# Thirty-two images through a fused network on one core: the first five turns written out in an order of their own, and the next to last pair normalised and scaled in three groups of tiles

## What is computed

```python
def forward(x, ...):                                  # token network, 192 channels, 14x14 patches
    loc = conv(x, pl_w, pl_b, stride=PATCH)
    loc = dwconv(gelu(loc), pl_dw, pl_pw, pl_pwb)     # layer "L"
    g = wavelet_packet(x)
    g = gelu(conv(g, pg_w1, pg_b1))
    g = gelu(dwconv(g, pg_dw, pg_pw, pg_pwb))         # layer "G"
    glob = conv(g, pg_w2, pg_b2)                      # "W2"
    gate = 0.5 * (jnp.tanh(alpha) + 1.0)
    h = (1.0 - gate) * loc + gate * glob
    h = jax.nn.relu(dwconv(h, f1_dw, f1_pw, f1_pwb))  # "F1"
    h = jax.nn.relu(dwconv(h, f2_dw, f2_pw, f2_pwb))  # "F2"
    h = dwconv(loc + h, f3_dw, f3_pw, f3_pwb)         # "F3"
    ...                                               # layer norm over the channels, class token in front
h = jnp.concatenate([tokens(x), txt], axis=1)         # 1 + 196 + 128 tokens of 192
h = h + attention(_layernorm(h))
h = h + ffn(_layernorm(h))

def attention(x):
    q = mlp(x, qw1, qb1, qw2, qb2)                    # k and v alike, gelu inside
    scores = jnp.einsum('bid,bjd->bij', q, k) / SCALE
    scores = scores * mask                            # 0 <= i - j < 64, no softmax
    y = jnp.einsum('bij,bjd->bid', scores, v)
    ...                                               # layer norm with ln_w, ln_b

def bitlinear(x, w, g):                               # used twice in the FFN: 192 -> 2x512, silu gate, 512 -> 192
    x_norm = rmsnorm(x, g)
    x_q = activation_quant(x_norm)                    # round(x * 127 / max|x|) per token
    return jnp.einsum('bsd,od->bso', x_q, weight_quant(w))   # weights -1, 0, 1 times a scale
```

## Time and profile before

| what | us |
| --- | --- |
| median of three runs | 1143.92 |
| lowest and highest | 1141.91, 1146.18 |
| the profiled execution, its own time | 1147.13 |
| its span in the profile | 1145.3 |

### The profile page before, as it was taken

One profiled execution on the slowest core, in us unless ns is written; L12 is line 12 of the kernel. 1 busy time (PEld: TensorE's weight loads), 2 busy tenths in 40 slices (PEclk: granted clock), 3 DMA queues, 4 the chain that ended last, 5 costly groups with the idle time before them and its releaser, 6 DMA issues.

```text
span 1145.3 us, 19061 instructions
## 1 busy us (share of the span) xinstructions
PE 1059.6 (93%) x5641; PEld 700.3 (61%) x5691; DVE 976.4 (85%) x2829; ACT 881.8 (77%) x2173; POOL 792.1 (69%) x916
## 2 busy tenths in 40 slices
PE   6887999999999999999999999999999989888865
PEld 4554667666757575766666675757676666454522
DVE  0678868999989898999999998989899999666786
ACT  3446758697979888898979798988889787738545
POOL 4245475878787787878787778877787887646334
PEclk9888999999999999999999999999999999979988
DMA  8111010101001010101010100101010000000000
GB/s 342 43 50 40 4 50 4 50 5 58 13 22 49 11 59 10 60 11 60 7 61 5 33 38 19 51 10 60 11 60 10 18 9 12 8 16 16 16 16 22
DMA packets 23687, 41.14 MB, mean 36 GB/s; under 512 B 3649, under 2 KB 20385, under 8 KB 21281
## 3 DMA queue, kind: packets, MB, share of 16 engines
q1 hardware_dynamic: 23584, 39.93, 10.3%
HBM read 31.02 MB, written 7.99 MB: 34 GB/s over the span
## 4 chain that ended last, share of the span: by engine, by line
PE 53%; ACT 22%; DVE 16%; issue 4%; POOL 3%; DMA 2%; SPq 1%; DVEq 0%; POOLq 0%; ACTq 0%
PE bank L558 10%; PE bank L590 4%; ACT xh L1265 4%; PE bank L592 3%; PE bank L601 3%; PE bank L652 3%; ACT y_sb L1274 3%; DVE bank L1953 3%; PE bank L600 3%; ACT early L1251 2%; PE bank L776 2%; PE bank L536 2%; PE bank L708 2%; PE bank L537 2%; PE bank L654 2%
## 5 line engine op out<-in xcount | busy, mean ns | idle before, releaser
L1953 DVE SCALAR_TENSOR_TENSOR bank<-padA,c_col,bank 128x406 f32<-128x406 f32 x560 | 358.5, 640 | 9.1
L558 PE MATMUL bank<-x_sb,w_emb 128*128 128x392 f32 x576 | 221.1, 513 | 6.1 <-ACT padA L1201 3.1
L1251 ACT ACTIVATE prod<-padB,c_col 128x196 f32<-128x196 f32 x432 | 175.4, 451 | 4.9 <-DVE padB L1965 3.9
L558 PEld LDWEIGHTS bank<-x_sb,w_emb 128*128 128x128 f32 x576 | 102.0, 194 | 64.1 <-issue 12.6
L3045 POOL TENSOR_TENSOR yg<-y_f,c_gout 128x512 f32<-128x512 f32 (+2 forms) x73 | 92.9, 1273 | 52.5 <-DVE y_f L2234 52.2
L1251 ACT ACTIVATE early<-padB,c_col 128x196 f32<-128x196 f32 x288 | 118.9, 449 | 3.7 <-POOL accB L3079 3.6
L536 PE MATMUL bank<-accA,w_sq 128*128 128x196 f32 x256 | 66.5, 341 | 11.8 <-POOL accB L3079 6.8
L2214 DVE SCALAR_TENSOR_TENSOR ya<-th,bank 128x512 f32<-128x512 f32 (+2 forms) x73 | 49.9, 684 | 28.7 <-ACT th L1323 27.4
L708 PE MATMUL bank<-w_in,xq 128*128 128x512 bf16 (+2 forms) x252 | 67.1, 382 | 5.1 <-ACT xq L1317 2.4
L590 PE MATMUL bank<-xT,w_sq 128*128 128x325 f32 x192 | 64.4, 447 | 4.0 <-ACT hq L1209 3.9
L3064 POOL TENSOR_TENSOR prod<-prod 128x392 f32<-128x392 f32 x48 | 48.9, 1018 | 27.8 <-ACT prod L1251 27.7
(11 more groups left out here) (320 smaller groups left out, 3015.7 us busy)
## 6 DMA issues: line engine op xcount, KB each, us to landing
x_sb<-xt SPq DMA_DIRECT2D x16, 1176.0 KB, 5.2
out<-o_sb SPq DMA_DIRECT2D x64, 96.0 KB, 1.9
w_sq<-squares SPq DMA_DIRECT2D x1, 3840.0 KB, 15.9
h_sb<-txt SPq DMA_DIRECT2D x32, 51.8 KB
out<-o_sb SPq DMA_DIRECT2D x32, 48.0 KB, 1.9
h_sb<-txt SPq DMA_DIRECT2D x32, 44.2 KB
w_in<-win SPq DMA_DIRECT2D x1, 1024.0 KB, 17.8
h<-h SPq DMA_DIRECT2D x16, 48.0 KB, 1.9
```

What stands on the lines that cost most here:

```text
L558: done = mm(pE[:, 0:2 * N_PATCH], w_emb[:, k, m, :], x_sb[:, k, :], start=k == 0, stop=k == KC - 1)
L1251: made = go(grid(prod[ACC[s] ^ 1][:, k, :]), tap_view(padB[min(s, 2)], SIDE, k), ACT.Copy, scale=tapcol(s, 1, k))
L1953: v.scalar_tensor_tensor(grid(acc if k == TAPS - 1 else run), tap_view(pad, ROWS_A, k), tapcol(s, 0, k), grid(run), ALU.mult, ALU.add).the ...
```

## The change

Three things are done.

First, the fixed list is no longer used for the first turns: `fill()` is a list of its own for turns 0 to 4 (0 to 2 on TensorE), and `all_turns` starts behind it. It holds the same calls. On TensorE `layer_L(0)` comes ahead of `query_key_weights()`, where it came behind it and behind four more embedding matmuls of pair 1, and the column sums of the weights come two chunks earlier. On ScalarE three outputs of the attention's first layers and `loc_out(2)` are ahead of a few products, and two key outputs ahead of an embedding output. On VectorE the statistics of the attention's input come three taps later, one tap comes ahead of `input_bn(1)`, and values and output statistics change places with a tap or more. On GpSimd two sums for pair 1 are ahead of those for pair 2, one of them ahead of `token_add(0, 0)`. On the sync engine text 0 is loaded ahead of image pair 2, and image pair 4 behind class token 1.

Second, pair 14 is treated as pair 15 was: `late(f)` takes the place of `last(f)` in the output norm and the token scales, and the waits count on from one pair to the next.

Third, `drain()` holds a new order on every engine. The steps of FFN tiles of pair 12 and 13 stand earlier against the attention of pairs 14 and 15, and `keep_busy` is spread in another way.

```diff
+LATE = PAIRS - 2
+def late(f):
+    return f >= LATE
...
             def join(f, par):
-                if last(f):
-                    sp.wait_ge(l_h2, 2)
+                if late(f):
+                    sp.wait_ge(l_h2, (f - LATE) * 3 + 2)
...
             def drain():
                 store(11, 1)
                 join(12, 0)
                 load_txt(14)
                 store(11, 2)
+                store(11, 3)
                 load_cls(14)
-                store(11, 3)
                 store(11, 4)
                 store(*last_tile(11))
+                store(12, 0)
                 join(13, 1)
                 load_txt(15)
-                store(12, 0)
-                load_cls(15)
                 store(12, 1)
                 store(12, 2)
+                load_cls(15)
...
+            def fill():
...
+                embed_chunk(1, EMB_BB, range(0, 2))
+                weight_totals()
+                embed_chunk(1, EMB_BB, range(2, 4))
+                layer_W2(0)
+                embed_chunk(1, EMB_BB, range(4, 6))
+                layer_L(0)
+                query_key_weights()
+                embed_chunk(1, EMB_GA, range(0, 2))
+                embed_chunk(1, EMB_GA, range(2, 4))
+                embed_chunk(1, EMB_GA, range(4, 6))
...
             pe.wait_ge(s_foldev, KC)
-            all_turns(turn, 17)
+            fill()
+            all_turns(turn, 3, 17)
             drain()
...
             def round_tokens(f, par, n):
-                if last(f):
-                    act.wait_ge(l_f, LF_STEPS * (1 if n < 2 else 2 if n in (3, 4) else 3))
+                if late(f):
+                    act.wait_ge(l_f, LF_STEPS * ((f - LATE) * 3 + (1 if n < 2 else 2 if n in (3, 4) else 3)))
```

On TensorE the end of the drain before pair 15's last tiles reads, of before and of the change, for example:

```diff
                 rounded_token_transposes(14, 1)
-                keep_busy(2)
                 rounded_hidden_transposes(14, 0)
                 ffn_in(14, 1)
                 ffn_out(14, 0)
-                keep_busy(2)
+                mixed_values(15, 0)
                 rounded_token_transposes(14, 2)
-                keep_busy(1)
+                mixed_values(15, 1)
                 ffn_in(14, 2)
-                keep_busy(14)
+                mixed_values(15, 2)
+                keep_busy(9)
                 rounded_hidden_transposes(14, 1)
```

1663 lines of the change are left out of this document (1118 added, 545 removed).

## The result

The changed kernel takes 1135.46 us (median of five, 1133.55 to 1136.65); the kernel before, run again beside it, 1141.91. The ratio is 0.9932, with a 95% interval from 0.9909 to 0.9954: 0.7% faster, some 8 us, in the forecast's range but with half of the gain that was worked out. The profiled execution has a span of 1133.7 us, 11.6 less than that of before.

What follows compares the result with a forecast made beforehand. The prediction took TensorE to bound the kernel from 121 to 916 us, with gains only ahead and behind. Its terms, 8.4 + 7.0 + 0 + 0.5 = 15.9, taken off 1143.92, gave 1128.0 us, range 1117 to 1142.

Steps and rivals of the forecast that it cites:

- What bounds it, and where the gain lies: TensorE bounds 121 to 916 us; gains lie at the weight product ahead and the join of pair 13 behind.
- The fill, 8.4: First turns: layer L(0) ahead of the weight product starts pair 0's mixing earlier; saves 8.4 us, between 4.0 and 9.4.
- I take full clock: the second part 4.5 us, half of 9.0: Weight product of query and key: after a 1.5 us pause its second part runs at full clock, 4.5 us.
- the 1.0 for layer F1(0): Fill: 1.0 us taken off since a longer pause can put this layer on half clock; between 0 and 2.3.
- The join of pair 13, 7.0: Drain: TensorE's 2.06 us wait and the half clock behind it go; saves 7.0 us, between 0 and 9.4.
- Pair 14 in groups, 0: Drain: work moved from GpSimd and ScalarE to VectorE cancels; net 0, between -8.0 and +5.4 us.
- the tiles done earlier, 0.5: About 1.7 more FFN tiles done before the last attention output; saves 0.5 us.
- The signs: Expected in the trace: pair 0's mixing near 57 (near 61 means B), clock 1.00 from 50 to 55, drain about 7.5 shorter.
- B: Rival: the weight product's second part stays at half clock; fill 4.0, drain 7.5, 1132.4 us; chance 0.12.
- A: Rival: the fill gains, the drain doesn't, its new order giving the gain back in other waits; 1135.5 us; chance 0.20.
- C: Rival: slower, pair 14's statistics and scales on VectorE set the pace of pair 13's FFN tiles; 1147.9 us; chance 0.08.
- E: Rival: the fill's shift is taken up in turns 2 to 4, only the drain's 7.5 left; 1136.4 us; chance 0.07.

Runs made afterwards that it cites:

- layer_only: Kernel before with one TensorE edit: layer L(0) ahead of the query and key weight product; ratio to the kernel before 0.9954.
- join_early: Kernel before with two sync engine lines exchanged: join of pair 13 ahead of the 24 stores of tile (11, 5); ratio 0.9963.
- fill_only: Kernel before with the changed first turns, `fill()`, on all five engines and nothing else of the change; ratio 0.9951.
- drain_only: Changed kernel with the first turns as before, leaving pair 14 in three groups and the new drain; ratio to the kernel before 0.9965.
- qk_late: emb_warm with the weight product's second part and copies behind F1(1)'s taps, 10 unused matmuls replacing 30, embedding chunk back in its old place; 1128.27 us, ratio 0.9868.
- warm_layers: Changed kernel with 11 unused matmuls ahead of layer F1(0) and 30 ahead of layer F1(1) on TensorE; ratio to the kernel before 0.9905.
- emb_between: Changed kernel with one embedding chunk of pair 1 moved between the two parts of the weight product; ratio to the kernel before 0.9899.
- emb_warm: Changed kernel with both the edit of emb_between and that of warm_layers; 1131.33 us, ratio to the kernel before 0.9888.
- before_again: Kernel before, no edit, traced a second time; one execution of 1140.27 us.
- old_drain_warm: Fill of emb_warm, old drain with the join of pair 13 ahead of the 24 stores, pair 14 as before; 1132.62 us, ratio 0.9903.
- late_old: old_drain_warm with pair 14's output norm and token scales in three groups, all else in the old order; 1139.05 us, ratio 0.9950.

## Why the forecast was half right, step by step

**What bounds it, and where the gain lies.** Right. The bound stretch hands a shift on unchanged, the two places named are the ones that carry the gain, and one edit of one or two lines at each (layer_only, join_early) gives it: 5.3 and 4.2 us. These add to 9.5, as fill_only and drain_only do (9.6); a kernel with just the two edits was not run. The whole change measured 7.8 (0.9932 of 1143.92), which its interval lets be 9.6. The sum had 15.9.

**The fill, 8.4.** The runs show 5.6, in the range of 4.0 to 9.4. The step that failed is the likeness to the pause of 1.55 us that left the clock at 1.00, and with it "I take full clock: the second part 4.5 us, half of 9.0". In the changed kernel the pause did leave it at 1.00, and the fall came inside the product; without a pause it came as well. The second part took 6.5 us in place of 4.5, of which an earlier start gave 0.3 back. Only 1.4 of these 2.0 are clock: "half of 9.0" was wrong too, since the product at full clock takes 5.15 (qk_late), its one-column matmuls not being twice as fast. The second mis-sized term is the 1.0 for layer F1(0), which was 2.7 against the first trace: above the 2.3 that I had set as its bound. It was not only the layer's clock, as I had it: 1.2 us of VectorE's wait stay at 1.00 (warm_layers), and they are gone when TensorE also does a chunk of embedding earlier, for which ScalarE waits ahead of the layer's products (emb_between, emb_warm). And as with the join, the 66.33 that the 9.4 is counted from was a slow execution's: the four traces with the old fill have the mixing at 66.3, 63.2, 64.5 and 65.5, the three with the plain new one at 58.6, 59.8 and 58.5, on average 5.9 earlier.

**The join of pair 13, 7.0.** The mechanism is right and the line is shown. The step that failed is the price of the half clock, "13.7 - 1.3 - 6.6 = 5.8" (the FFN product in it is 1.48 by the earlier trace rows, not 1.3). It was taken from one execution: in before_again the same values and scores take 9.0 us behind the same waits, and not 13.7. Against the first trace join_early has 6.6, against the other 4.4, and in the ratio 4.2. The whole new drain gives 4.0 where the sum had 7.5. What I lacked was a second look at the same stretch, and the page gave a hint that I used only for arithmetic: the profiled execution was 3.2 us above the median. A wait that repeats to 0.01 us can have a price that does not.

**Pair 14 in groups, 0, and the tiles done earlier, 0.5.** The sum of the two came out near: 1.3 us by the medians of old_drain_warm and emb_warm, 1.3 by the table (288.8 us from pair 11 to the end in the changed kernel, 290.1 in join_early), and nothing by the ratios of drain_only and join_early. But adding them as two terms was wrong in kind. The forecast let 66% of 8.0 us lie on the path wherever it stood. It depends on the place: in one piece ahead of tile (13, 0) it cost 6.4, in three pieces it gave 6.8. The way from 14 to 15 became 4.9 us longer in the changed kernel (52.15 against 47.2, the mean of two traces), and from 15 to the end 6.6 shorter. Why the one grew and the other shrank was not tested by itself.

**The signs and the rivals.** The mixing started at 58.6, between the 57 and the 61 of the signs, with the clock at 0.80 and 0.50 where 1.00 was the sign; the joined tile made nobody wait, the scores of 14 ran at 1.00, and from pair 11 to the end it is 7.0 and 4.9 us shorter than in the two traces of before. B came true for the fill in part (6.5 us, between its 9.0 and 4.5). A is not what the runs show, since the drain gives its 4.0 on its own. C's mechanism exists, and late_old shows it, but the changed kernel's order avoids it. E fell: the shift reached the bound stretch.

## What to carry to other kernels

Look for work on the critical engine that merely stands behind something long and wants nothing from it: seven matmuls moved, and two lines of DMA order exchanged, each measured as much as the rewritten lists of five engines around them. Before a stall's price is put in a sum, split it into the wait, which repeats, and the clock behind it, which doesn't: the second has to be the mean of several executions. Time a stretch at full clock where a run has it, before halving what it took at half. And a change that regroups work and one that reorders the work around it are not two terms; price them together, at the place where they meet.

## What the hardware showed that I had not expected

- TensorE fell to its lower level (1.2 of 2.4 GHz) without any pause ahead of it: in the run of ten one-column products and the embeddings behind, with TensorE busy for 2.00 of every 2.00 us (emb_between, 1.00 up to 54, then 0.72 and 0.50). It did so in all five traces in which the product follows on other work at that place, and behind it at the other place (qk_late, 1.00 up to 98, then 0.54). That it is the one-column matmuls in it was not tested alone.
- The same program at the same waits had clocks of 0.50 and 0.91 in the same window of the drain; this, with the like of it in the fill (4.7 us by the start for pair 11, 2.2 from 11 to 14), is the 6.9 us between two executions. With the unused matmuls and the embedding in the pause, four traces had pair 11 at 839.1 to 841.0, where four with the old fill had 844.8 to 849.5. The times of whole kernels are not steadier for it in general: 1.0 and 1.4 us apart in warm_layers and emb_warm, but 3.7 to 4.8 in the four kernels run later with unused matmuls in the fill.
- Eleven and thirty unused matmuls, in front of two layers of 2.3 us each, put the start of the bound stretch 2.5 us earlier (842.4 against 844.9, one trace each; the ratios, 0.9905 against 0.9932, have intervals that touch).
- The same run of eight records with one column took 2.13 us at 0.50 and 1.31 at 1.00, a factor of 1.6 and not 2 (before, qk_late); the eight with 192 columns had 3.81 and 2.05, a factor of 1.9.
